# A selective scan's read-out on TensorE: one contraction behind every step, or two behind every second

## The reference

```
h = exp(dt_t * A) * h + dt_t * B_t * x_t        state, per (b, e, n)
y_t = sum over n of h * C_t                     read-out, per (b, e)
```

## Time and profile before

| | us |
|---|---|
| median of 3 runs | 1314.23 |
| lowest, highest | 1314.06, 1314.28 |
| span of the profiled execution | 1313.7 |
| first stage (to the first decay of the scan) | 219.7 |
| the 16 bodies | 1063.9 |
| tail | 30.1 |

### The profile page before, as it was taken

The page is one execution under the profiler, slowest core; times in us unless marked ns, Lnnn a source line. Parts: engine busy times, 40 slices in busy tenths (PEclk is TensorE's granted clock), DMA queues, the critical chain, the costliest instruction groups (busy, mean ns, idle before and its releaser), DMA issues. The chain is left out here.

```text
span 1313.7 us, 32989 instructions
## 1 busy us (share of the span) xinstructions
PE 1229.1 (94%) x10152; PEld 734.2 (56%) x10152; DVE 1066.0 (81%) x2254; ACT 1017.2 (77%) x1748; POOL 864.3 (66%) x1217
## 2 busy tenths in 40 slices
PE   4999964899999999999999999999999999999998
PEld 2666742345555555555555555555555655565556
DVE  4578774998888888888888888888888888888884
ACT  1667654898888888888888888888888888888881
POOL 5355443887676767676777676767777676767671
PEclk9898975999999999999999999999999999999999
DMA  4022234111111111110101111111111111111100
GB/s 120 33 101 99 100 132 136 35 30 34 34 34 30 38 30 34 30 32 31 32 28 31 30 32 29 31 30 30 28 30 32 32 32 32 32 32 32 33 5 8
DMA packets 73366, 56.47 MB, mean 43 GB/s; under 512 B 43488, under 2 KB 62816, under 8 KB 70240
## 3 DMA queue, kind: packets, MB, share of 16 engines
q1 hardware_dynamic: 73312, 55.79, 14.0%
HBM read 36.38 MB, written 19.40 MB: 42 GB/s over the span
## 5 line engine op out<-in xcount | busy, mean ns | idle before, releaser
L803 POOL TENSOR_TENSOR decayed<-decay,state 128x256 f32<-128x256 f32 x1024 | 727.0, 731 | 309.2 <-DVE state L1102 287.8
L1043 ACT ACTIVATE decay<-ps,a_col 128x512 f32<-128x512 f32 x1024 | 651.2, 691 | 108.1 <-PE ps L860 106.4
L1102 DVE TENSOR_TENSOR state<-decayed,ps 128x256 f32<-128x256 f32 x1024 | 392.0, 417 | 109.5 <-PE ps L926 96.2
L860 PE MATMUL ps<-moving,dt_pick 96*128 96x256 bf16 x2048 | 393.4, 273 | 8.5 <-DMA moving<-dt_stage 8.1
L1093 DVE TENSOR_TENSOR ps<-decay,ps 128x512 f32<-128x512 f32 x512 | 353.7, 691 | 48.0 <-PE ps L902 29.1
L1055 ACT COPY state<-ps 128x512 f32<-128x512 f32 x512 | 302.2, 590 | 70.0 <-issue 58.0
L884 PE MATMUL ps<-state,c_cols 128*32 128x256 f32 x4096 | 327.0, 391 | 0.0
L860 PEld LDWEIGHTS ps<-moving,dt_pick 96*128 96x128 bf16 x2048 | 197.2, 98 | 80.7 <-issue 9.2
L902 PE MATMUL ps<-moving,b_rows 96*128 96x256 bf16 x1024 | 196.1, 273 | 24.7 <-DVE ps L1093 22.6
L926 PE MATMUL ps<-moving,b_rows 96*128 96x256 bf16 x1024 | 201.5, 278 | 7.7 <-DVE state L1102 6.1
L926 PEld LDWEIGHTS ps<-moving,b_rows 96*128 96x128 bf16 x1024 | 58.7, 97 | 213.4 <-issue 180.5
(11 more groups left out here) (122 smaller groups left out, 1001.0 us busy)
## 6 DMA issues: line engine op xcount, KB each, us to landing
moving<-u_stage SPq DMA_DIRECT2D x32, 576.0 KB
moving<-dt_stage SPq DMA_DIRECT2D x32, 192.0 KB
b_stage<-b_parts SPq DMA_DIRECT2D x24, 192.0 KB, 2.5
b_rows<-b_stage SPq DMA_DIRECT2D x256, 18.0 KB
dt_stage<-dt_parts SPq DMA_DIRECT2D x8, 512.0 KB, 2.8
u_stage<-u_parts SPq DMA_DIRECT2D x8, 512.0 KB, 3.2
dt_stage<-dt_parts SPq DMA_DIRECT2D x8, 256.0 KB, 2.1
u_stage<-u_parts SPq DMA_DIRECT2D x8, 256.0 KB, 2.3
```

What stands on the lines that cost most here:

```text
L803: nc.gpsimd.tensor_tensor(decayed[:, p], decay[:, k % RING, p * E:(p + 1) * E], state[:, (k - 1) % RING, p * E:(p + 1) * E], ALU.mult).the ...
L860: m = nc.tensor.matmul(ps[:, DTP + q // 2, (q % 2) * E:(q % 2 + 1) * E], dt_pick[:, q, :], moving[:, cb, kk, :], start=True, stop=True)
L1043: nc.scalar.activation(decay[:, k % RING, f * SELF:(f + 1) * SELF], ps[:, DTP + f, :], ACT.Exp, scale=a_col[:, 2:3]).then_inc(ready, 1)
L1102: nc.vector.tensor_tensor(state[:, k % RING, p * E:(p + 1) * E], decayed[:, p], ps[:, SELFP, p * E:(p + 1) * E], ALU.add).then_inc(self_st ...
```

## The change

TensorE's step loses the case distinction. The SBUF half's product of k + 1 always comes right behind the second spread. The contraction is left out in even steps, and in odd ones those of k - 3 and k - 2 follow the product, one behind the other. The two contractions after the last body are as before (even ones are done in an odd step three later, odd ones two later, so 30 and 31 are left over). All waits inside `contract` and `self_product` stay as they are, and no other engine's program changes.

```diff
                         m.then_inc(acc_state, 1)
                         spread_acc(i, k + 2)
-                        if k % TC == LAG:
-
-                            self_product(i, k + 1)
+                        self_product(i, k + 1)
+                        if k % 2 == 1:
+
+                            contract(i, k - LAG - 1)
                             contract(i, k - LAG)
-                        else:
-                            contract(i, k - LAG)
-                            self_product(i, k + 1)
                         finish_groups(finish, i, k)
```

## The result

The changed kernel takes 1328.98 us, the median of 4 runs (1327.37 to 1329.52), beside 1314.26 for the kernel before on the same chip (4 runs, 1314.06 to 1315.54): a ratio of 1.0105, 95% interval 1.0091 to 1.0119. It is 14.7 us slower, where 15.1 us less were forecast.

The account below looks back on a forecast made before the run. TensorE was taken to set the pace in quiet steps. Thirteen bodies gaining 1.15 us each, plus 1.0 (last) and 0.7 (second), less 1.6 (first), took 15.1 off 1314.23: 1299 us, forecast 1290 to 1309, range 1284 to 1316.

Parts of the forecast that it names:

- part (2): TensorE's steps become uneven, so VectorE's chain takes half the saving: quiet pair 3.86 to 3.87 us against 3.98, gain 0.11.
- The chain of 3.86: Quiet pair from SBUF product through contractions, finishing matmuls, VectorE's decay and adds to the next such product: 3.86 us.
- part (3): VectorE's even adds wait for the pair's first contraction, done 1.00 us after the SBUF product's start instead of 0.43.
- my walk: Full body timed by pairs: steps 10 to 14 8.28, 14 to 16 4.49, all others 53.34, together 66.1 us.
- (1): TensorE contractions paired: 1.00 plus 0.09 to enter, against 1.32; 0.23 us saved a pair, 59 in all if nothing else binds.
- The cover that I named: VectorE's even adds end at 1.75 and its decay is due at 2.46: 0.7 us of cover, enough in quiet steps.
- (4): Steps 10 to 14 take 8.28 us for 8.37, 14 to 16 4.49 for 3.98, all others 53.34 for 55.05.
- (5): First body costs 1.6 us, its pairs taking 3.42 against 3.29; the second body gains about 0.7.
- rival (b): The contraction's count comes at 1.43, making quiet pairs 3.94 us and a body 68.25: 1329 us, chance 0.10.
- (c): A pair of contractions takes as long as two single ones, 0.14 us more: 1331 us, chance 0.05.
- (a): TensorE's saving arrives whole, as stalls stay as they are: 1255 us, anything up to 1285, chance 0.10.

Follow-up runs that it names:

- a bf16 matmul behind the pair: Changed kernel with the even step's dt spread issued one step sooner, between the two contractions and the finishing matmuls: 1316.16 us, ratio 1.0009.
- both together: Changed kernel with the dt spread between contractions and finishing matmuls, and eight state buffers for the SBUF half: 1308.49 us, ratio 0.9945.
- the pairing alone: Changed kernel with the two contractions kept in odd steps but the SBUF half's product behind them again: 1292.43 us, ratio 0.9835.
- eight buffers: Changed kernel with eight state buffers instead of four for the SBUF half, so VectorE's adds wait for contraction t-8: 1320.48 us, ratio 1.0038.
- the parity turned: Changed kernel with VectorE's placing of C one step later, in odd steps (k % 16 == 11 for 10): 1317.53 us, ratio 1.0016.
- the order alone: Changed kernel with one contraction in every step, always behind the SBUF half's product: 1333.67 us, ratio 1.0138.

## Why the prediction was wrong

**The step that failed is in part (2):** "the finishing matmuls and the spread follow", priced at 0.67 (0.45 + 0.22). That price is from the earlier trace rows, where a bf16 product stands between the contraction and the float32 matmuls. Part (2) moves this product away and keeps its row's price. The price behind a contraction was in my own rows: in the earlier trace rows the float32 matmuls behind the two contractions have 0.70, not 0.60. I used that row for the pair's 1.00 and passed over its second line. It stood in the scan of the kernel before as well, in the two steps of a body in which the product is issued ahead of the contraction; there two float32 matmuls hold the issue for 0.53:

```profile
788.26 0.64 PE L884 MATMUL ps<-state,c_cols 128*32 128x256 f32 x8
788.83 0.70 PE L1002 MATMUL ps<-h,w 128*128 128x256 f32 x2
789.36 0.38 PE L860 MATMUL ps<-moving,dt_pick 96*128 96x256 bf16 x2
```

The chain of 3.86 became 3.96, and since 3.98 was before, nearly the whole gain of a quiet pair was gone. By the runs this step is the largest part of the miss and not all of it: a bf16 matmul behind the pair takes back 12.6 us of the 29.8 (with what else its move does), the count of part (3) is 8.8, both together 21.0, and 8.8 are left in the uneven places.

Pair by pair against my walk (16 pairs of a body, from one even PSUM product to the next, 66.1 in all before the 0.15 that I added; measured 67.9): thirteen pairs are 0.04 to 0.11 over it and 12 to 14 0.02, together 1.24; steps 14 to 16 0.22 (4.71 for 4.49); 18 to 20 0.32 (4.76 for 4.44). The spread behind the pair took 0.09 off in each of seven pairs, what the walk lacked there to within 0.02; that much is the float32 exit, shown. In 0 to 2, 2 to 4 and 10 to 12 it brought nothing back, and what is over there isn't explained; in 6 to 8 and 22 to 24 its new place cost something itself. In 14 to 16 the walk had the instant right: the second add of step 14, released by GpSimd, comes 4.08 behind the PSUM product of step 12 (783.05 to 787.13); what is over arises behind it. In 18 to 20 the second add of step 19 stands for GpSimd and comes 0.59 behind the first, where the walk had 0.33, and that is 0.26 of the 0.32 (read, not tested):

```profile
796.60 0.42 DVE L1100 TENSOR_TENSOR state<-decayed,ps 128x256 f32<-128x256 f32 x1
...
797.19 0.42 DVE L1100 TENSOR_TENSOR state<-decayed,ps 128x256 f32<-128x256 f32 x1 [0.17 <-POOL decayed L803]
```

The miss of 29.8 us is then: thirteen full bodies at 67.9 for 66.25, 21.6; the first two bodies at 64.3 and 66.3 for 61.5 and 63.7, 5.4; the last at 63.8 for 62.3, 1.5; the rest, 1.3, isn't in the bodies (the profiled execution began them 1.9 sooner than the one before did, and took 1.6 less than the median).

By the prediction's parts:

(1) *Switches:* right. A pair is issued in 1.00 to 1.01 in all kernels and places that I read, and the kernel with the pairing alone turned it into time, 3.73 for a quiet pair. By the rule of the Trainium skill ("TensorE: Matmul & The Clock Gate", Packing small matmuls) it would be 1.14, an estimate from that rule and the 0.57 of the earlier trace rows; no run here agrees with it. But a switch has two ends, and I priced only the one into the contraction (0.09) and took the one out of it as free. It is all but free into bf16 (0.23 for the next product, against 0.22) and costs 0.10 into float32.

(2) *Order:* each link of the chain within 0.01 but the one above. That VectorE's chain eats half the saving was right (3.87 with the exit out, against 3.75 by TensorE's issue), and it binds with the product in front and not with the pair in front (3.73).

(3) *Count:* the adds go 1.08 to 1.09 behind the product, not 1.00. The cover that I named holds in quiet steps of full bodies: eight buffers bring nothing there, and 0.24 in steps 10 to 12, where C is placed. In the first body it doesn't: there I took the chain through VectorE, 3.42, for the longest, though my own terms for the loop through GpSimd (1.00 + 0.56 + 1.42 + 0.05 + 0.48) make 3.51. With 1.09 for 1.00 they make 3.60; measured 3.58.

(4) *Uneven places:* 10 to 14 came to 8.40 (8.28), 14 to 16 to 4.71 (4.49), 18 to 20 to 4.76 where I counted on a gain of 0.4 on 4.84. That placing C is dearer in an even step was right, and set much too low (0.1 in step 10, 0.3 in 26 to 28): with the parity turned a body is 0.73 shorter. The reason given, adds that wait for the contraction, is only 0.24 of it.

(5) *First bodies:* forecast +1.6 and -0.7, measured +4.4 and +1.9. The sum was wrong by itself: 3.42 against 3.29 is 0.13 a pair, 2.1 and not 1.6. In the first body, which has no finishing matmuls and so no exit to pay, eight buffers take 3.2 of the 4.4 away, and 0.7 is a stretch at the lower clock (below). In the second, the buffers bring 0.5 and the spread behind the pair 0.8.

**The rivals.** The time came out at 1329, the number of rival (b), and 2 under that of (c), but neither mechanism did it. (b) would have had the count come at 1.43 and quiet pairs held by it; it comes at 1.08, and its removal leaves them at 3.96. (c) would have had the pair take 1.14; it takes 1.00. That the number fits is chance. The idea of (b), that the count costs, did hold in the first body, by 3.2 us. (a) would have had quiet pairs at 3.75; they have 3.96, and 3.87 with the exit out. What no case held was a price on leaving the contraction. Nor did the range, 1284 to 1316, leave room for one: I had counted 0.1 us a pair as settled because its row was exact, and 0.1 us in 16 pairs of 16 bodies is 26 us.

## What to carry to other kernels

When an instruction is moved, price anew what comes to stand behind its old and its new neighbours: a row's duration holds for the order it was read in, and a row in which the new order already occurs, however rare, outweighs a hundred of the old. Where switching between kinds of work costs an engine something, as here, group the odd kind and let the successor that pays least come behind it. And if every second step becomes long, put the long step where the engine that feeds it is late (here the product behind the pair, the extra work of VectorE in odd steps); in this kernel both together gained 3%, where the same grouping in the other order, with C where it was, lost 1%.

## What the runs showed of the hardware

A float32 matmul of full 128 x 128 weights behind a contraction of 128 x 32 tiles: two of them issue in 0.53 to 0.54 us with a length of 0.70, against 0.43 to 0.44 and 0.60 behind bf16, for two different lines (L1000 in the changed kernel and L975 in the order alone), and for one behind a single contraction in the kernel before (L1002). A bf16 matmul there pays 0.01 at most (0.23 to the next start, against 0.22), and saves it for the float32 one behind it. The Trainium skill ("TensorEngine Tiling (Array Packing)", Key Properties) has it that changing the tiling mode drains TensorE. The 0.09 into the contraction agrees with that; that the way out costs a float32 matmul and not a bf16 one, it does not tell, and no run here shows the reason.

The granted clock had one stretch at the lower level in the middle of the changed kernel's first body (windows, clock in the third column from the end):

```profile
250.00:256.60 6.60, 4.70 (x42) 2.11 (x41) 5.69 (x12) 5.10 (x10) 4.45 (x7) 1.00 0.27 95
256.60:260.10 3.50, 3.50 (x24) 1.52 (x25) 2.48 (x4) 2.05 (x4) 2.36 (x4) 0.52 0.28 64
260.10:270.00 9.90, 8.80 (x88) 4.13 (x89) 8.31 (x17) 9.18 (x17) 8.07 (x11) 1.00 0.05 13
```

For 3.5 us it was 0.52, 1.2 GHz, after 6.6 us in which TensorE was busy for 4.7. The changed kernel and six of the others had one such stretch in the first body of their profiled execution; the kernel before and the other six had none. It falls on different steps, and costs what the pair there takes longer, by VectorE's decays: in the changed kernel steps 20 to 22 have 5.43, where the kernel with the spread behind the pair has 4.77; that one has it in steps 28 to 30, 4.80 for 3.37. So it is 0.7 to 1.4 us, a part of what the first body lost, for which the forecast had no term.
